# Layer-norm and RMS-norm inverse roots taken by GpSimd as powers of -0.5, in a one-core adaLN, decayed-attention and MoE layer

## The reference, cut to what matters

```python
mod = (silu(c) @ wmod).reshape(2, 6, 1, 256)            # sa, ca, ga, sb, cb, gb; ga and gb kept at least 0.25 in size
h = layernorm(x) * (1 + ca) + sa                        # x: 2 x 1024 x 256;  layernorm = (x - m) / sqrt(var + 1e-5)
q, k, v, u = split(h @ W_qkvu.T)                        # 16 heads of 16; q, k = silu(q), silu(k)
o = linear_attention(q, k, v)                           # decay exp(-s*distance), running state, per head
o = u * o * rsqrt(mean(o * o) + 1e-6)                   # RMS norm over 256
x = x + ga * (o @ W_out.T)
h = layernorm(x) * (1 + cb) + sb
x = x + gb * (top2_of_8_experts(h) + shared_expert(h))  # each: silu(h @ gate.T) * (h @ up.T) @ down.T, FF = 512
```

## Time and profile before

| | us |
|---|---|
| time, median of 3 runs | 373.6 |
| span of the profiled execution, first to last instruction | 371.5 |
| time less span (what lies around the span) | 2.1 |
| PE busy / DVE / ACT / POOL in the span | 361.5 / 280.9 / 217.7 / 197.4 |
| table loads on ACT, each | 1.28, seven of them |
| granted TensorE clock, whole span | 1.000 |

### The profile page before, as it was taken

One profiled execution on the slowest core, in us unless ns is written; L12 is line 12 of the kernel. 1 busy time (PEld: TensorE's weight loads), 2 busy tenths in 40 slices (PEclk: granted clock), 3 DMA queues, 4 the chain that ended last, 5 costly groups with the idle time before them and its releaser, 6 DMA issues.

```text
span 371.5 us, 12942 instructions
## 1 busy us (share of the span) xinstructions
PE 361.5 (97%) x4978; PEld 314.9 (85%) x4983; DVE 280.9 (76%) x566; ACT 217.7 (59%) x457; POOL 197.4 (53%) x193
## 2 busy tenths in 40 slices
PE   8989998999999989999999999999999999999996
PEld 5546555788888879899999999999999999999995
DVE  6996388999999985679986887776778685555543
ACT  5688667687777855647357656565565634333222
POOL 2000003977888776122274687878677666674250
PEclk9999999999999999999999999999999999999999
DMA  7953031000198008989434465665757686665543
GB/s 262 379 78 48 2 131 41 2 4 30 41 380 151 30 31 311 347 305 250 109 91 90 112 114 91 106 111 87 118 99 94 106 104 89 104 113 76 71 58 114
DMA packets 53043, 45.35 MB, mean 122 GB/s; under 512 B 31524, under 2 KB 46996, under 8 KB 52856
## 3 DMA queue, kind: packets, MB, share of 16 engines
q1 hardware_dynamic: 43048, 32.09, 31.3%
q0 software_dynamic: 7488, 10.27, 19.0%
q10 hardware_dynamic: 2448, 2.18, 2.2%
HBM read 27.60 MB, written 10.49 MB: 103 GB/s over the span
## 4 chain that ended last, share of the span: by engine, by line
PE 69%; POOL 12%; DVE 7%; issue 5%; ACT 4%; DMA 1%; ACTq 0%; POOLq 0%; DVEq 0%
PE ps L1638 37%; PE ps L1656 18%; PE ps L1420 7%; POOL tmp L558 2%; POOL tmp L579 2%; PE ps L1406 2%; POOL tmp L562 2%; POOL tmp L577 2%; POOL wx L567 2%; POOL h2s L583 2%; DVE st L942 1%; DMA tmp<-in_decay_tables 1%; DVE tmp L959 1%; PE ps L1541 1%; ACT tmp L734 1%
## 5 line engine op out<-in xcount | busy, mean ns | idle before, releaser
L1638 PE MATMUL ps<-tmp,wx 128*128 128x128 bf16 x1776 | 105.5, 219 | 0.0
L1638 PEld LDWEIGHTS ps<-tmp,wx 128*128 (+1 forms) x1776 | 102.2, 98 | 0.9 <-issue 0.2
L615 POOL DMA_INDIRECT out<-tmp,dk x39 | 69.2, 1775 | 39.5 <-SPq L519 35.2
L862 ACT ACTIVATE tmp<-tmp 128x512 bf16<-128x512 f32 x55 | 34.6, 629 | 81.3 <-PE ps L1656 61.2
L1656 PE MATMUL ps<-wx,tmp 128*128 (+1 forms) x660 | 80.8, 273 | 0.2 <-DVE tmp L1267 0.2
L1656 PEld LDWEIGHTS ps<-wx,tmp 128*128 128x128 bf16 x660 | 62.2, 98 | 7.0 <-DVE tmp L1267 0.5
L1261 DVE TENSOR_TENSOR tmp<-ps,tmp 128x512 f32<-128x512 f32 x55 | 37.9, 689 | 36.0 <-PE ps L1638 31.3
L610 POOL DMA_INDIRECT tmp<-h2rows,src_i x39 | 43.5, 1116 | 16.7 <-issue 10.7
L1638 PE MATMUL ps<-w_hl,wx 128*128 128x128 bf16 x864 | 51.3, 219 | 0.5 <-ACT tmp L851 0.5
L1638 PEld LDWEIGHTS ps<-w_hl,wx 128*128 (+1 forms) x864 | 49.6, 98 | 1.1 <-issue 0.6
L1267 DVE TENSOR_TENSOR tmp<-tmp 128x512 bf16<-128x512 f32 x55 | 38.3, 696 | 10.7 <-ACT tmp L862 10.6
(11 more groups left out here) (196 smaller groups left out, 554.8 us busy)
## 6 DMA issues: line engine op xcount, KB each, us to landing
wx<-in_wexp SPq DMA_DIRECT2D x26, 512.0 KB, 5.2
xres<-in_x SPq DMA_DIRECT2D x4, 512.0 KB, 6.8
h2rows<-h2s ACTq DMA_DIRECT2D x16, 128.0 KB, 3.8
out<-h2s SPq DMA_DIRECT2D x12, 128.0 KB
h2s<-in_wmod SPq DMA_DIRECT2D x1, 1024.0 KB, 9.3
wx<-decay_rows SPq DMA_DIRECT2D x16, 64.0 KB
modr<-mod_rows SPq DMA_DIRECT2D x1, 1024.0 KB, 4.6
wx<-in_wqkvu SPq DMA_DIRECT2D x1, 768.0 KB, 7.0
```

Source lines behind the costliest of these rows:

```text
L615: e.indirect_dma_start(t["out"], bass.IndirectOffsetOnAxis(ap=dst_i[:, j:j + 1], axis=0), yb[(NA + j) % 2], None, compute_op=ALU.add).then ...
L862: e.activation(hs[p][:, 0:FF], hf[p], ACT.Copy).then_inc(s["inner_high"], 1)
L1638: ins = e.matmul(half(bank, m * P), weight(at_, weights(part, w) + k * FF + m * P, P), xT[f % NXT][:, (2 * a + k) * P:(2 * a + k + 1) * P] ...
```

## The change

The inverse root leaves ACT and DVE. GpSimd adds epsilon and raises to the power of -0.5 with a tensor of constants (`minus_half`). For the second norm it forms the shift as well. ACT keeps an Identity that takes the mean of squares plus epsilon out of PSUM (GpSimd has no access to PSUM there). ACT's Sqrt instructions are gone, and with them three table loads: one Silu load stands at the head, and Exp and Silu around the softmax stay. The last tile's normalised rows come from ACT like the others'.

```diff
 GpSimd, head
+            e.memset(minus_half[:], -0.5).then_inc(s["half_set"], 1)
+            def ln1_factors(i):
+                e.wait_ge(s["ln1_moments"], GT * (i + 1))
+                e.tensor_scalar(rs1[:, 0, part], mv1[:, part, 1], LN_EPS, None, ALU.add)...        # ln1_biased
+                e.wait_ge(s["ln1_biased"], i + 1)
+                e.tensor_tensor(rs1[:, 1, part], rs1[:, 0, part], minus_half[:], ALU.pow)...       # ln1_inverse
+                e.wait_ge(s["ln1_inverse"], i + 1)
+                e.tensor_tensor(rs1[:, 2, part], mv1[:, part, 0], rs1[:, 1, part], ALU.mult)...    # ln1_shift
+            for i in range(NT // GT):
+                ln1_factors(i)
 GpSimd, step_attention(n), m = n - 3
+                if mine(m):
+                    wait(e, "rms_taken", m + 1)
+                    e.tensor_tensor(rs2[:, q, 1:2], rs2[:, q, 0:1], minus_half[:, 0:1], ALU.pow)...  # rms_inverse
                 if mine(h):
                     ... (L558, L562)
+                if mine(m):
+                    wait(e, "ln2_moments", m + 1)
+                    wait(e, "ln2_rows", m - 1)
+                    e.tensor_scalar(rs2[:, q, 2:3], mv2[:, q, 1:2], LN_EPS, None, ALU.add)...        # ln2_biased
+                    wait(e, "ln2_biased", m + 1)
+                    e.tensor_tensor(rs2[:, q, 3:4], rs2[:, q, 2:3], minus_half[:, 0:1], ALU.pow)...  # ln2_inverse
+                    e.tensor_scalar(rs2[:, q, 5:6], mv2[:, q, 0:1], -1.0, None, ALU.mult)...         # ln2_signed
+                    wait(e, "ln2_inverse", m + 1)
+                    wait(e, "ln2_signed", m + 1)
+                    e.tensor_tensor(rs2[:, q, 4:5], rs2[:, q, 5:6], rs2[:, q, 3:4], ALU.mult)...     # ln2_shift
                 if mine(w, NSTATE):
                     ... (L567, then L577, L579, L583)
 ScalarE
-                    e.activation(rs2[:, m % 2, 2:3], mv2[:, m % 2, 1:2], ACT.Sqrt, bias=epst[:, 0:1])...
-                    e.activation(rs2[:, (m + 1) % 2, 0:1], half(OUT_BANK, D, 1), ACT.Sqrt, scale=1.0 / D, bias=epst[:, 1:2])...
+                    e.activation(rs2[:, (m + 1) % 2, 0:1], half(OUT_BANK, D, 1), ACT.Identity, scale=1.0 / D, bias=rms_eps[:])...
-                if m == NT - 1:
-                    e.activation(silu_back[:], epst[:, 0:1], ACT.Silu)
-                elif mine(m):
+                if mine(m):
                     ... (L781)
-            e.activation(rs2[:, 0, 0:1], epst[:, 0:1], ACT.Sqrt)
-            ln1_root((0,))
+            e.activation(silu_back[:], rms_eps[:], ACT.Silu)
-            ln1_root((1,))
-            ln1_root((2, 3))
 VectorE
-                e.reciprocal(rs1[:, 1, part], rs1[:, 0, part])...          # and the shift of the first norm
-                    e.reciprocal(rs2[:, q, 1:2], rs2[:, q, 0:1])...        # RMS norm
-                    e.reciprocal(rs2[:, q, 3:4], rs2[:, q, 2:3])...        # second norm, and its shift
-                if m == NT - 1:
-                    ... (L1126, the last tile's rows)
```

More of the change, by code:

```diff
@@ L543, in _ @@
         def _(e):
+            e.memset(minus_half[:], -0.5).then_inc(s["half_set"], 1)
             for par in range(2):
                 e.memset(zeros_beside(0, par), 0.0).then_inc(s["values_zeroed"], 1)
+            e.wait_ge(s["half_set"], 1)
+            def ln1_factors(i):
+                part = slice(GT * i, GT * (i + 1))
+                e.wait_ge(s["ln1_moments"], GT * (i + 1))
+                e.tensor_scalar(rs1[:, 0, part], mv1[:, part, 1], LN_EPS, None, ALU.add).then_inc(s["ln1_biased"], 1)
+                e.wait_ge(s["ln1_biased"], i + 1)
+                e.tensor_tensor(rs1[:, 1, part], rs1[:, 0, part], minus_half[:], ALU.pow).then_inc(s["ln1_inverse"], 1)
+                e.wait_ge(s["ln1_inverse"], i + 1)
+                e.tensor_tensor(rs1[:, 2, part], mv1[:, part, 0], rs1[:, 1, part], ALU.mult).then_inc(s["ln1_shift"], 1)
+            for i in range(NT // GT):
+                ln1_factors(i)
             e.wait_ge(s["mod_rows"], 16)
@@ L663, in _ @@
             e.activation(dk[:, :, :], slr.unsqueeze(2).to_broadcast([P, NH, DH]), ACT.Exp, scale=minus_left).then_inc(s["key_decay_made"], 1)
[L665 to L670, removed]
+            e.wait_ge(s["eps_set"], 1)
             def weights_high(c):
@@ L773, in step_attention @@
                     wait(e, "out_product", m + 2)
-                    e.activation(rs2[:, (m + 1) % 2, 0:1], half(OUT_BANK, D, 1), ACT.Sqrt, scale=1.0 / D, bias=epst[:, 1:2]).then_inc(s["rms_root"], 1)
-                if m == NT - 1:
-                    e.activation(silu_back[:], epst[:, 0:1], ACT.Silu)
-                elif mine(m):
+                    e.activation(rs2[:, (m + 1) % 2, 0:1], half(OUT_BANK, D, 1), ACT.Identity, scale=1.0 / D, bias=rms_eps[:]).then_inc(s["rms_taken"], 1)
+                if mine(m):
                     wait(e, "ln2_shift", m + 1)
@@ L914, in _ @@
         def _(e):
-            e.memset(epst[:, 0:1], LN_EPS).then_inc(s["eps_set"], 1)
-            e.memset(epst[:, 1:2], RMS_EPS).then_inc(s["eps_set"], 1)
+            e.memset(rms_eps[:], RMS_EPS).then_inc(s["eps_set"], 1)
             e.memset(idle_operand, 0.0).then_inc(s["idle_zeroed"], 1)
@@ L948, in normalise @@
                 g = token_group(i)
[L949 to L954, removed]
                 wait(e, "ln1_shift", i + 1)
@@ L959, in normalise @@
                     e.tensor_scalar(xn[:, n % (2 * GT), :], xres[:, GT * g + j, :], rs1[:, 1, n:n + 1],
[L960 removed]
+                                    rs1[:, 2, n:n + 1], ALU.mult, ALU.subtract).then_inc(s["ln1_rows"], 1)
             def first_inputs():
@@ L1536, in outputs @@
                 wait(e, "x1_made", r)
-                wait(e, "rms_root", r)
+                wait(e, "rms_taken", r)
                 for k in range(KD):
```

33 lines of the change are left out of this document (13 added, 20 removed).

## The result

The changed kernel takes **396.85 us** (median of four runs, 396.63 to 397.6), the kernel before beside it 373.74 (373.26 to 374.09): a ratio of 1.0618, 95% interval 1.0601 to 1.0634. The forecast was 379.4 with a range up to 387. The sign was right, the size was off by a factor of four: +5.8 forecast, +23.1 measured. The profiled span goes from 371.5 to 395.0 us, +23.5. Ratios leave out the disturbed executions, over 1.5% slower than the fastest of their kernel, which the medians keep, so the two can differ (experiment 7).

A forecast was written before the change was run, and what follows sets the result against it. POOL's list, 5.53 us per attention step, was to become the bound. Step 3 +2.1, eleven periods +4.0, step 15 +0.2 and the last load -0.5 gave +5.8: 379.4 us against 373.6, range 373.8 to 387.0.

The forecast's parts named there:

- What bounds the kernel: Attention steps 4 to 14: POOL's list grows from 4.26 to 5.53 us, above PE's 5.03, and becomes the bound.
- The savings on DVE and ACT: Attention steps: DVE loses 0.46 us and ACT 0.28 per step, which buys nothing as both have room in 5.53.
- the expert stretch: From 162 us on, PE nearly always busy: as long as before, only starting later; 0 us added.
- What a small POOL instruction costs: Prices at 128x1 on POOL: plain 0.15 us, or 0.26 with result awaited; power 0.30, bounds 0.15 and 1.78.
- Rival 2: Powers on POOL are a software routine, 0.6 us each, list 6.13 us per step: +13.6, time 387; chance 0.14.
- The prediction's other estimate: POOL's five small instructions per step at 0.3 us instead of 0.19, by the skill's rule: +0.55 a step, time near 386.
- Eleven periods: +4.0: Attention steps 4 to 14: POOL's list gains 1.27 us, period 5.53, eleven of them against 56.82 us: +4.0 us.
- Step 3: +2.1: Once: the RMS power stands behind `scale_down` on POOL, the residual is 1.4 us late, step 4's first product +2.1 us.
- The head: 0: First norm at the start: POOL's factors ready at 7.72 against 7.78 us, later groups within 0.1: 0 us.
- Covered: First norm's later groups and first Silu load lie in the 22 to 61 us window where PE is full: 0 us.
- Step 15: Last of the list-bound attention steps, without L567: POOL's list 4.84 us against 4.66 before, +0.2 us.
- The -0.5 for the last load: Silu load at 147.19 us removed: PE's gate product, which had waited 0.50 us, starts earlier; -0.5 us.

The follow-up runs named there:

- experiment 7: Kernel before with every Sqrt turned into Identity, the head's load into Silu, so three table loads go: 372.78 against 373.79 us, ratio 0.997 when measured again.
- experiment 1: Changed kernel with its three powers turned into products, norms being other numbers: 384.24 us, ratio 1.0304.
- experiment 2: Changed kernel with the second norm's sign issued ahead of the power, between epsilon and power: 393.82 us, ratio 1.0542.
- experiment 3: Changed kernel with one more 128x1 power on POOL at the end of each step from 4 on, read by nobody: 403.73 us, ratio 1.0796.
- experiment 6: Changed kernel with only the first norm back on ACT's root and DVE's reciprocal: 397.3 us where the kernel before took 376.23, ratio 1.056.
- experiment 11: Kernel before with POOL powers only for tiles 14 and 15 (RMS: 15) and Silu's load moved to step 17: 373.25 against 373.79 us, ratio 0.9983.
- experiment 8: Kernel before with only the RMS norm's root and reciprocal made a power on POOL: 377.29 us where the kernel before took 376.23, ratio 1.0012.
- experiment 9: Changed kernel with DVE's weight split in eight steps turned from a two-input subtraction into a one-input copy: 394.8 us, ratio 1.0569.

## Why the prediction was wrong in size

**What bounds the kernel: right.** POOL waits for nobody in steps 5 to 14, DVE waits for the RMS power in front of the residual, PE and ACT wait for POOL, and the expert stretch is unchanged. The savings on DVE and ACT buy nothing, as said. Experiments 1 to 3 move the list by three different amounts (quiet periods of 5.58, 6.16 and 6.93 us instead of 6.41), and the time follows each.

**The step that failed: "What a small POOL instruction costs".** The plain price held: a product fills 0.14 to 0.15 us, 0.27 with its result awaited (0.26 forecast). The power was put at 0.30 (0.34 to its result) and costs 0.54 (0.65). I had stated 1.78 as the upper bound and took a value next to the lower one, "since 128x1 is one element on each partition". A product's row says nothing on a power's work per element. Rival 2, with a chance of 0.14, nearly had the price (0.6); its reason, a routine in software, no run shows. The prediction's other estimate, 386 with every small instruction at 0.3 us, came nearer than 379.4 by luck, since a plain product does last 0.19.

**"Eleven periods: +4.0" became +15.8.** The list grew by 2.15 us, not 1.27. From start to start in the step above:

| | forecast | measured |
|---|---|---|
| RMS power | 0.30 | 0.54 |
| L581 to the epsilon, beyond the old 0.69 | 0 | 0.11 |
| epsilon | 0.26 | 0.31 |
| power to sign | 0.30 | 0.66 |
| sign to shift | 0.26 | 0.40 |
| shift | 0.15 | 0.14 |

The two powers are 0.60 of the missing 0.88. The rest is three small things: the epsilon, a TENSOR_SCALAR, starts 0.08 after the end of the instruction before it, where a TENSOR_TENSOR that waits for nothing starts 0.04 before it; epsilon and sign last 0.23, not 0.19; and the shift waits for a power and for the sign. 4.26 + 2.15 = 6.41 is the quiet period. Eleven are 70.5; six of them hold a split. Five of these are 0.32 to 0.35 longer, and step 14 is 0.44 longer, as there the split meets L606 (1.12 us at 150.33, 0.67 elsewhere). That is 2.1 more: 72.6 against 72.61 measured and 56.82 before. This contention was not in the forecast. It is also why rival 2's 387 is about 10 us short, though its price was right: it had only the two powers dearer, and neither the head, nor the contention, nor the 0.28 us a step of the three small things.

**Step 3: +2.1 became +3.5, and half of its reason falls.** The delay of the power behind `scale_down` (L593 before, L622 after) is real. But moving `scale_down` behind the steps that follow (experiment 5) doesn't help, since POOL then stands in the idle time before the moments all the same; giving POOL that work within the idle time (experiment 4) gains 1.4 us. What costs is that POOL's queue waits empty-handed for the moments:

```profile
71.93 1.29 POOL L622 TENSOR_TENSOR h2s<-h2s,modr 128x512 f32<-128x512 f32 x1
73.17 0.56 POOL L573 TENSOR_TENSOR rs<-rs,minus_half 128x1 f32<-128x1 f32 x1
73.77 0.48 DVE L1095 SCALAR_TENSOR_TENSOR xres<-ps,rs,xres 128x256 f32<-128x256 f32 x1 [1.70 <-POOL rs L573]
75.02 0.23 POOL L585 TENSOR_SCALAR rs<-mv 128x1 f32<-128x1 f32 x1 [1.28 <-DVE mv L1101]
80.77 0.72 POOL L577 TENSOR_TENSOR tmp<-tmp,modr 128x256 f32<-128x256 f32 x1
```

DVE's residual waits 1.70 us, forecast 1.4. Beyond that the size is the price of the powers again, and one L608 at 1.07 (77.97 us), beside DVE's split.

**The head: 0 became +2.35.** A power of 128x4 was taken for 0.41 us with its wait and takes 1.03 to 1.06 in the first three groups (1.13 to the next start) and 1.40 in the fourth. The groups' rows come in turn, so it adds up over the first two: the first group's rows start at 8.77 instead of 7.78, the second's at 18.26 instead of 15.92. The second group in the changed kernel:

```profile
16.25 0.57 POOL L553 TENSOR_SCALAR rs<-mv 128x4 f32<-128x4 f32 x1 [7.51 <-DVE mv L959]
16.91 1.05 POOL L555 TENSOR_TENSOR rs<-rs,minus_half 128x4 f32<-128x4 f32 x1
18.03 0.20 POOL L557 TENSOR_TENSOR rs<-mv,rs 128x4 f32<-128x4 f32 x1
```

Its epsilon lasts 0.57 us where the first group's lasted 0.24; a split of DVE (L1002, 16.07 to 16.73) runs beside it. That contention is the likely reason: the epsilon is 0.57 in the second and fourth groups, beside an L1002, and 0.23 to 0.24 in the first and third, without one. No run took it away. It is 0.33 us of the +2.35. Experiment 6 shows that the head's loss is whole at the gate. "Covered" was read off the 22 to 61 us window, but this group stands ahead of it.

**Step 15 and the gate.** +0.2 became +1.4 by the same dearer list (period 6.06). The -0.5 for the last load was right in itself, as experiments 7 and 11 show (-0.66 and -0.46 by the marks). In the changed kernel PE still waits 0.34 us for the gate's Silu at 172.78, and the rest is eaten by the powers in steps 16 to 19, where the list is short but the chain from residual to rows runs through them.

**What stays open:** why the stretch behind the gate is longer on the other chip; how the time lost to contention follows from inputs and from overlap; how much of the head's +2.35 is one execution against another; and whether the transfer that PE waits for at 177 us takes back what an earlier gate gives.

## What to carry to other kernels

Before work goes to the engine with the least room, add up that engine's list in the new state and price an operation the trace has never shown by running it once; a tile of one element is no sign that it is cheap. An engine's idle gap may be what keeps its transfers or reads apart from another engine's, so ask what used to run beside the gap. Work is free only within the slack of the step that gets it: one power per step cost the steps nothing, though 0.8 us once where POOL had no slack; beyond the slack each cost its full 0.54 us; and the only gain of the idea, 0.2%, lay in the two steps that had room. An instruction that starts earlier may also meet a transfer that has not landed, so follow the trace behind the wait that was removed.

## What the runs showed of the hardware

- A power on POOL (changed kernel): 0.57 us at 128x1, 1.03 to 1.06 at 128x4, so about 0.16 us for each further element; a product 0.19 and 0.20. Beside a DVE instruction with two SBUF inputs the 128x1 power took 1.08 (experiment 8) and the 128x4 power 1.40 (fourth group of the head).
- On POOL a TENSOR_SCALAR starts 0.07 to 0.09 us after the end of the instruction before it, whether that is of its own kind (experiment 2) or not; a TENSOR_TENSOR that waits for nothing starts 0.04 before that end.
- POOL's 128x256 product beside a DVE instruction with two SBUF inputs, 0.47 us of overlap: 1.06 us instead of 0.73, and that one 1.03 instead of 0.68. Beside one with one input, 0.21 us of overlap: 0.79 (experiment 9).
- A table load of 1.28 us placed in ACT's idle time costs nothing that the marks show (two of the three in experiment 7); three loads gone are worth 0.3%.
